# Three graph hops on one core: part of the row gather moved from GpSimd to SyncE, with a shorter ring of buffers

## The chip, the core and the metric

The program runs on one core of a Trainium2 chip. The core has TensorE (PE; its weight loads are listed as PEld), VectorE (DVE), ScalarE (ACT), GpSimd (POOL) and SyncE (SP), each with its own instruction stream; they meet through semaphores, and data moves between HBM and SBUF by DMA. The metric is device time of one execution, the median of several runs.

## The reference, cut to what matters

Four graph layers on 6250 nodes of 128 features and 100000 edges run one after the other. The first one holds the three hops of this case: a weighted sum over edges, three times (`Kh` is 4), each from the result of the last.

```python
edge_index = jnp.stack([src, dst])
row, col = (edge_index[0], edge_index[1])
def spmm(z):
    return jax.ops.segment_sum(edge_weight[:, None] * z[col], row, num_segments=N)
z = x
y = z @ weights[0]
for k in range(1, Kh):
    z = spmm(z)
    y = y + z @ weights[k]
return y / jnp.sqrt(jnp.asarray(d, dtype=x.dtype))
x = _layernorm(x + _L0_gnn_ref(x, edge_index, edge_weight, L0_gnn_weights), axis=-1)
```

Three attention layers follow, in which the destination-sorted and the source-sorted edge lists are used again.

## The kernel before, in words

**Lists.** The program first sorts the edges by `src` on the chip (`histogram`, `place_edges`, `scatter_edges`, `read_edges`). The sorted list is cut into chunks of 128 edges: 784 chunks (`CU`), of which 782 hold edges, in 196 groups of four (`GU`, `G`). `o.gather` holds, for each chunk, the node whose row each of its 128 edges needs. On the side of the sums there are 832 columns (`CH`) in 208 groups (`GROUPS`): a chunk that spans two blocks of 128 nodes is used by two columns. `o.chunk` says which chunk a column uses, `o.slot` where its rows lie in the ring, `o.need` up to which group of chunks it must have landed, and `o.free` how many groups of columns must be summed before a group of chunks is no longer needed.

**A hop** (`hop`, called three times) has five streams:

- POOL (L1117 to L1129) walks the 196 groups and issues four indirect DMAs in each, one a chunk: 128 rows of 512 bytes into one of 64 places of `rows`, a ring of 16 groups (`RING`). From group 16 on it first waits on `freed` for the group that held the place before.
- SP (L1314 to L1321) waits for each group to land (`got`), raises `landed` by one, and, from group 8 on, loads a number from `o.free`, waits on `summed` for the group eight back, and raises `freed`.
- PE (`a_round`, L1165 to L1190) waits for `landed` and for the weighted one-hot matrices, and multiplies four columns into PSUM.
- DVE makes these matrices (`weigh`, L1213) and adds the products to the block sums (`add`, L1226).
- In the first hop PE and DVE also count the keys of the second sort; in the second and third they also rank edges for it (`rank`), in the first 200 and 192 groups of columns.

```python
for n in range(GU):
    s = n % RING
    if n >= RING:
        pool.wait_ge(freed, n - RING + 1)
```

At the end of a hop DVE joins two half sums and SP stores the new table. The second hop's POOL stream then issues 16 scatter DMAs (L1136). After the third hop POOL goes straight on with the scatter of the second sort (`scatter_ranked`, L1355, 768 DMAs), beside the dense part of the first layer, and the list is read back after them.

**Order.** Each engine's order is the program's own; no planner sets it. Between the first sort and the scatter all engines meet at a block's end, and a hop starts behind such a meeting too: POOL begins its gathers right behind it, while PE, DVE, ACT and SP of the first two hops first finish a stage that they share the block with (`meet`, L75, and L1310 for SP).

Of the kernel before, what the change touches and what calls it, by code (L numbers as in the profile page):

```python
# [5 lines left out]
ALU = mybir.AluOpType  # L6
# [41 lines left out]
assert PAD_STEP * (CH - 1) + PAD_SKIP * (P - 1) < N  # L48
AFTER = NSLOT - E
assert TU * QU == CU and RING * G == 64 and NBLK < (RING - 2) * G  # L50

# [424 lines left out]
def place_edges(nc, k, counts, first_place, o, name, stack, shared):  # L476
# [18 lines left out]
    block_f = sb("block_f", [P, CH])  # L495
    row_i = sb("row_i", [1, CH], I32)
    need_i = sb("need_i", [1, GROUPS], I32)
    starts = ps("starts", [HIS, 1])
# [31 lines left out]
    def _(dve):  # L530
        steps = [0]

        def chain(ins):
            ins.then_inc(d, 1)
            steps[0] += 1
            dve.wait_ge(d, steps[0])
# [29 lines left out]
        nc.vector.tensor_scalar(o.block_base[:], block_f[:], float(P), None, ALU.mult)  # L566
        chain(nc.vector.tensor_copy(row_i[:], o.chunk[0:1, :]))
        chain(nc.vector.tensor_single_scalar(need_i[:], row_i[:, G - 1:CH:G], 2, ALU.arith_shift_right))
        nc.vector.tensor_single_scalar(o.slot[:], row_i[:], RING * G - 1, ALU.bitwise_and)
        nc.vector.tensor_scalar(o.need[:], need_i[:], 1.0, None, ALU.add)  # L570
        chain(nc.vector.tensor_single_scalar(block_f[:], block_f[:], float(NBLK - 1), ALU.min))
# [270 lines left out]
def read_edges(nc, k, table, o, name, stack, banks, shared):  # L842
# [23 lines left out]
    listed = sem("listed")  # L866
    limited = sem("limited")
    counted = sem("counted")
    counted_row = sem("counted_row")
# [11 lines left out]
    @shared.sync  # L881
    def _(sp):
        for h in range(2):
            here = slice(h * here_q, (h + 1) * here_q)
            sp.dma_start(lst[:, here, :], rows[:, here, :]).then_inc(loaded[h], 16)

    @shared.tensor
# [125 lines left out]
def hop(nc, k, o, table_in, table_out, name, tally=None, rank=None, shared=None, listed=None, early=None):  # L1013
# [3 lines left out]
    with ExitStack() as ctx:  # L1017
        sb, ps, sem = tools(nc, k, ctx, name)
        total = sb("total", [P, NBLK, D])
        odd = k.x[:, 0:NBLK, :]  # L1020
        rows = sb("rows", [P, RING * G, D])
        weighted = sb("weighted", [P, SLOTS, G, P])
        sums = ps("sums", [P, 2, G, D])
        got = [sem(f"got{s}") for s in range(RING)]
        landed = sem("landed")
# [4 lines left out]
        stored = sem("stored")  # L1030
        freed = sem("freed")
        running = sem("running")
        placed = sem("placed")
# [83 lines left out]
        def _(pool):  # L1117
            if listed is not None:
                pool.wait_ge(listed, 2)
            for n in range(GU):  # L1120
                s = n % RING
                if n >= RING:

                    pool.wait_ge(freed, n - RING + 1)
                    pool.sem_inc(running, 1)
                for g in range(G):
                    c = n * G + g
                    nc.gpsimd.indirect_dma_start(rows[:, s * G + g, :], None, table_in,  # L1128
                                                 bass.IndirectOffsetOnAxis(ap=o.gather[:, c:c + 1], axis=0),  # L1129
                                                 ).then_inc(got[s], 16)  # L1130
# [10 lines left out]
        def _(pe):  # L1141
# [26 lines left out]
            def a_round(i, first, ranks):  # L1168
                for s in range(DEEP):
                    b = s % 2  # L1170
                    n = i * DEEP + s
                    slots = load_blocks(nc, pe.engine, o.slot[:, bass.ds(n * G, G)], G, RING * G - 1)
                    need = pe.value_load(o.need[:, bass.ds(n, 1)], min_val=1, max_val=GU)
# [136 lines left out]
        @block.sync  # L1310
        def _(sp):
            home = table_out.rearrange("(b p) f -> p b f", p=P)
            for n in range(GU):
                sp.wait_ge(got[n % RING], (n // RING + 1) * 16 * G)  # L1314
                sp.sem_inc(landed, 1)  # L1315
                if n >= RING // 2 and n + RING // 2 < GU:

                    reader = sp.value_load(o.free[:, n - RING // 2:n - RING // 2 + 1], min_val=SLOTS + 1, max_val=GROUPS + SLOTS)
                    sp.wait_ge(summed, reader)
                    sp.sem_inc(freed, 1)  # L1320
            for n, here in enumerate(pieces):  # L1321
                sp.wait_ge(joined, n + 1)
                sp.dma_start(home[:, here, :], total[:, here, :]).then_inc(stored, 16)
            sp.wait_ge(stored, 16 * len(pieces))
# [1808 lines left out]
def graph_network(nc, a, out):  # L3133
    k = Shared()
    k.semaphores = []
    with ExitStack() as ctx:
# [17 lines left out]
        for o, n in ((by_src, "src"), (by_dst, "dst")):  # L3154
            o.place = sb(f"{n}_place", [P, CH + SPARE])
            o.begins = sb(f"{n}_begins", [P, CH], BF16)

            by_chunk = sb(f"{n}_by_chunk", [33, CH + SPARE], I32)
            o.block, o.within = by_chunk[0:1, :], by_chunk[32:33, :]
            o.sorted = dram(f"{n}_sorted", [LEAD + NSLOT + BEHIND, 4])  # L3160
            o.breaks = dram(f"{n}_breaks", [NSLOT + MOST_WCH * P], BF16)
        by_src.gather = sb("src_gather", [P, CU], I32)
        by_src.slot, by_src.need = sb("src_slot", [1, CH], I32), sb("src_need", [1, GROUPS], I32)
        by_src.free = sb("src_free", [1, 2 * P], I32)
        by_dst.typed = sb("dst_typed", [P, CH + SPARE], I32)
        by_dst.other = sb("dst_other", [P, CH + SPARE], I32)
# [10 lines left out]
        with ExitStack() as sort:  # L3177
# [8 lines left out]
            by_src.chunk_no = sort.enter_context(nc.sbuf_tensor("src_chunk_no", [P, QU], F32))  # L3186
            by_src.chunk = sort.enter_context(nc.sbuf_tensor("src_chunk", [P, CH], F32))
            with ExitStack() as unsorted:
                keys = unsorted.enter_context(nc.sbuf_tensor("keys", [P, 2, CH], F32))
# [142 lines left out]
```

## Time and profile before

| | |
|---|---|
| median of 3 runs | 9749.5 us (9728.2 to 9752.75) |
| profiled execution | 9737.26 us, span of the trace 9735.5 us |
| POOL busy | 6993.0 us, 72% of the span |
| DVE busy | 6539.5 us, 67% |
| PE busy | 6374.2 us, 65% |
| gathers of the three hops on POOL | 784 each |
| first gather of each hop | 1169.8, 2172.3 and 3185.0 us |

Register, branch, semaphore and DMA-issuing instructions of SP are not counted as busy, so SP has no line in the table of engines; its instructions are found by their lines. A POOL gather is counted as busy for the time in which POOL writes its DMA, not until the rows have landed. Idle time whose end is put down to "issue" is time in which an engine waited for nothing that the profile shows.

### The profile page before, as it was taken

The numbers are of one execution on the slowest core, as the hardware profiler recorded it, in microseconds if no ns is written. First come the engines' busy times: TensorE is split into PE (matmuls) and PEld (weight loads), VectorE is DVE, ScalarE is ACT, GpSimd is POOL, SyncE is SP. The second block draws the span as 40 slices with busy tenths as digits, with TensorE's granted clock in tenths as the row PEclk, the third lists the DMA queues.
The fourth block names the chain that finished last, engine by engine and source line by source line (L and its number), as shares of the span: only waits on it lengthen the run. The fifth ranks groups of instructions, "written<-read, shape, count | busy, mean of one in ns | idle before, by whom it ended". The sixth has DMA issues, their size and how long they took to land. (4 is left out here: it accounts for less than half of the span.)

```text
span 9735.5 us, 171552 instructions
## 1 busy us (share of the span) xinstructions
PE 6374.2 (65%) x37681; PEld 5551.4 (57%) x37682; DVE 6539.5 (67%) x22695; ACT 2118.1 (22%) x6216; POOL 6993.0 (72%) x7418
## 2 busy tenths in 40 slices
PE   6777655547666577639404666767776688876666
PEld 5666544436655566634204666556675578766665
DVE  7555566668777777736305888877777666667777
ACT  5222100001111111112101222232222222223333
POOL 7777777767777777777776777547775577767775
PEclk7555555556666655569756888889999665667777
DMA  0000012122212212234303333222222322223333
GB/s 25 2 2 2 18 53 52 53 61 53 53 53 55 57 53 53 53 77 146 100 2 86 104 104 104 87 47 55 55 55 55 100 54 54 54 72 108 108 108 97
DMA packets 436037, 614.74 MB, mean 63 GB/s; under 512 B 176561, under 2 KB 312069, under 8 KB 435109
## 3 DMA queue, kind: packets, MB, share of 16 engines
q0 software_dynamic: 257024, 486.93, 19.6%
q1 hardware_dynamic: 178305, 119.49, 4.3%
q8 instruction: 183, 3.00, 0.1%
q10 hardware_dynamic: 292, 3.41, 0.1%
q14 instruction: 233, 1.91, 0.1%
HBM read 520.17 MB, written 89.19 MB: 63 GB/s over the span
## 5 line engine op out<-in xcount | busy, mean ns | idle before, releaser
L1179 PE MATMUL hop_sums<-hop_rows,hop_weighted 128*128 x4992 | 1152.1, 403 | 1053.2 <-SPq L1315 674.4
L1128 POOL DMA_INDIRECT hop_rows<-hops,k_src_gather x1568 | 1483.3, 946 | 486.8 <-issue 477.6
L1179 PEld LDWEIGHTS hop_sums<-hop_rows,hop_weighted 128*128 128x128 f32 x4992 | 989.6, 295 | 1158.8 <-issue 1158.7
L1505 POOL DMA_INDIRECT l_pass_rows<-left_table,k_dst_other x832 | 796.2, 957 | 433.2 <-issue 244.6
L1505 POOL DMA_INDIRECT l_pass_rows<-related,k_dst_typed x832 | 788.6, 948 | 308.6 <-issue 238.7
L1505 POOL DMA_INDIRECT l_pass_rows<-key_table,k_src_gather x784 | 744.3, 949 | 365.9 <-issue 234.8
L2000 POOL DMA_INDIRECT l_weigh_rows<-row_table,l_weigh_ring x832 | 790.0, 949 | 297.9 <-issue 213.1
L728 POOL DMA_INDIRECT src_sorted<-src_scatter_records,src_scatter_places x784 | 753.1, 961 | 260.4 <-issue 188.2
L1355 POOL DMA_INDIRECT dst_sorted<-rec,dst_places x768 | 752.8, 980 | 237.2 <-issue 237.2
L1128 POOL DMA_INDIRECT hop_rows<-in_x,k_src_gather x784 | 742.4, 947 | 249.0 <-issue 238.7
L1213 DVE TENSOR_SCALAR hop_weighted<-k_numbers,k_src_place,src_weight 128x128 f32<-128x128 f32 x2496 | 850.1, 403 | 15.7 <-issue 8.7
L1521 ACT CAST l_pass_onehot_t<-l_pass_turned 128x512 f32<-128x512 bf16 x624 | 365.7, 586 | 2158.6 <-PE l_pass_turned L1569 2110.8
L1600 PE MATMUL l_pass_sums<-l_pass_zero 128*128 128x272 bf16 (+1 forms) x1210 | 235.7, 279 | 465.2 <-DVE l_total L1694 322.0
L1582 PE MATMUL l_pass_own<-l_right,l_pass_onehot_t 128*128 x1664 | 359.0, 299 | 257.7 <-DMA l_pass_rows<-left_table,k_dst_other 243.8
L1610 PE MATMUL l_pass_sums<-l_pass_terms,l_pass_onehot_f 128*128 128x136 f32 x3232 | 513.1, 308 | 1.1 <-DVE l_pass_terms L1877 1.1
L664 PE MATMUL src_scatter_nexts<-src_scatter_next_sb,src_scatter_oh_lo_t 128*128 128x50 f32 x1568 | 494.2, 425 | 0.0
L1106 ACT COPY hop_next_sb<-hop_next_ps 128x50 f32<-128x50 f32 x784 | 158.1, 202 | 1522.6 <-PE hop_next_ps L1151 1516.5
L1610 PEld LDWEIGHTS l_pass_sums<-l_pass_terms,l_pass_onehot_f 128*128 128x128 f32 x3232 | 472.1, 217 | 26.3 <-issue 3.2
L2018 PE MATMUL l_weigh_own<-l_keys,l_weigh_onehot_t 128*128 x1672 | 321.5, 352 | 229.9 <-ACT l_weigh_onehot_t L1970 229.9
L1814 DVE TENSOR_REDUCE l_pass_scores<-l_pass_pair 128x32 f32<-128x512 f32 (+1 forms) x624 | 426.2, 683 | 14.5
L1582 PEld LDWEIGHTS l_pass_own<-l_right,l_pass_onehot_t 128*128 128x128 f32 x1664 | 267.1, 202 | 289.7 <-issue 289.7
L2018 PEld LDWEIGHTS l_weigh_own<-l_keys,l_weigh_onehot_t 128*128 128x128 f32 x1672 | 272.4, 247 | 274.6 <-issue 274.6
(477 smaller groups left out, 17048.9 us busy)
## 6 DMA issues: line engine op xcount, KB each, us to landing
related<-l_tables_rows SPq DMA_DIRECT2D x50, 1024.0 KB, 4.5
hop_rows<-hops,k_src_gather POOLq DMA_INDIRECT x1568
l_pass_rows<-related,k_dst_typed POOLq DMA_INDIRECT x832
l_pass_rows<-left_table,k_dst_other POOLq DMA_INDIRECT x832
l_weigh_rows<-row_table,l_weigh_ring POOLq DMA_INDIRECT x832
src_sorted<-src_scatter_records,src_scatter_places POOLq DMA_INDIRECT x784, 2.1
hop_rows<-in_x,k_src_gather POOLq DMA_INDIRECT x784, 2.5
dst_sorted<-rec,dst_places POOLq DMA_INDIRECT x784
```

Source lines behind the costliest of these rows:

```text
L664: nc.tensor.matmul(nexts[:, b, g, 0:HIS], oh_lo_t[:, b, g, :], next_sb[:, g % 2, :], start=True, stop=True).then_inc(looked, 1)
L728: nc.gpsimd.indirect_dma_start(table, bass.IndirectOffsetOnAxis(ap=places[:, s, g:g + 1], axis=0), records[:, s, g, :], None).then_inc(sen ...
L1128: nc.gpsimd.indirect_dma_start(rows[:, s * G + g, :], None, table_in, bass.IndirectOffsetOnAxis(ap=o.gather[:, c:c + 1], axis=0),).then_in ...
L1179: last = nc.tensor.matmul(sums[:, b, g, :], weighted[:, s % SLOTS, g, :], rows[:, bass.ds(slots[g], 1), :], start=True, stop=True)
L1213: last = nc.vector.tensor_scalar(weighted[:, s, g, :], k.numbers, o.place[:, c], o.weight[:, c], ALU.is_equal, ALU.mult)
L1355: nc.gpsimd.indirect_dma_start(table, bass.IndirectOffsetOnAxis(ap=places[:, c:c + 1], axis=0), rec[:, c, :], None).then_inc(sent[c % SLOT ...
L1505: nc.gpsimd.indirect_dma_start(rows[:, s, g, :], None, table, bass.IndirectOffsetOnAxis(ap=index[:, c:c + 1], axis=0),).then_inc(got[s], 16)
L1582: last = nc.tensor.matmul(own[:, b, g, :], onehot_t[:, b, g, :], spread[:, bass.ds(blocks[g], 1), :], start=True, stop=(att is None))
L1610: last = nc.tensor.matmul(into[:, bass.ds(within[g], 1), 0:width], onehot_f[:, m % 2, g, :], term, start=False, stop=False, skip_group_che ...
L1814: nc.vector.tensor_reduce(mine, pair[:, b, :, :, :].rearrange("p (s t) h f -> p s t h f", t=per), AX.X, ALU.add).then_inc(scored, 1)
L2000: nc.gpsimd.indirect_dma_start(rows[:, s, g, :], None, table, bass.IndirectOffsetOnAxis(ap=ring[:, s, g:g + 1], axis=0),).then_inc(got[s], 16)
L2018: last = nc.tensor.matmul(own[:, b, g, :], onehot_t[:, b, g, :], spread[:, bass.ds(blocks[g], 1), :], start=True, stop=True)
```

## The change: what it does

In each hop, chunks 752 to 763 (groups 188 to 190, `AT_SIDE` to `BEHIND_SIDE`) are no longer gathered by POOL. Their 1536 rows are loaded by SP with one DMA of 512 bytes for each row, into 12 places of their own (`SIDE`) behind the ring. The node numbers for it are copied once, behind the first sort, from `o.gather` by way of HBM into one partition (`o.side`), and SP loads eight of them into registers at a time (`AT_ONCE`): a "part". There are 192 parts a hop: two behind each of groups 0 to 7 (`AHEAD`), then one behind each of groups 8 to 183. POOL also leaves out the last two chunks, which hold no edge: 770 gathers in place of 784. The ring has 8 groups in place of 16 (`NEAR`), and SP frees a group four behind the one that landed, not eight. `place_edges` works out a second table of places, `o.hop_slot`, for PE in the hops.

```diff
+CHUNKS = -(-E // P)
+NEAR = 8
+SIDE = 12
+AT_SIDE = 188
+BEHIND_SIDE = AT_SIDE + SIDE // G
+AT_ONCE = 8
+AHEAD = 8
...
-        chain(nc.vector.tensor_copy(row_i[:], o.chunk[0:1, :]))
+        chain(nc.vector.tensor_copy(row_i[:], o.chunk[:]))
...
+        chain(nc.vector.tensor_single_scalar(aside[:], row_i[:], AT_SIDE * G, ALU.is_ge))
+        chain(nc.vector.tensor_single_scalar(behind[:], row_i[:], BEHIND_SIDE * G, ALU.is_ge))
+        chain(nc.vector.tensor_tensor(aside[:], aside[:], behind[:], ALU.subtract))
+        chain(nc.vector.tensor_single_scalar(o.hop_slot, row_i[64:65, :], NEAR * G - 1, ALU.bitwise_and))
+        nc.vector.scalar_tensor_tensor(out=o.hop_slot, in0=aside[64:65, :], scalar=float(NEAR * G - AT_SIDE * G % (NEAR * G)),
+                                       in1=o.hop_slot, op0=ALU.mult, op1=ALU.add)
...
+        sp.wait_ge(listed, 2)
+        sp.dma_start(o.side_home, o.gather[:, AT_SIDE * G:BEHIND_SIDE * G]).then_inc(side_in, 16)
+        sp.wait_ge(side_in, 16)
+        sp.dma_start(o.side[:], o.side_home.rearrange("(a p) c -> a (p c)", a=1)).then_inc(side_in, 16)
+        sp.wait_ge(side_in, 32)
...
-        rows = sb("rows", [P, RING * G, D])
+        rows = sb("rows", [P, NEAR * G + SIDE, D])
...
-            for n in range(GU):
-                s = n % RING
-                if n >= RING:
-
-                    pool.wait_ge(freed, n - RING + 1)
+            for n in [*range(AT_SIDE), *range(BEHIND_SIDE, GU)]:
+                s = n % NEAR
+                if n >= NEAR:
+
+                    before = n - NEAR if not AT_SIDE <= n - NEAR < BEHIND_SIDE else n - 2 * NEAR
+                    pool.wait_ge(freed, before + 1)
                     pool.sem_inc(running, 1)
-                for g in range(G):
+                for g in range(min(G, CHUNKS - n * G)):
...
+            order = [(p, c) for p in range(P) for c in range(SIDE)]
+            used = [0] * NEAR
             for n in range(GU):
-                sp.wait_ge(got[n % RING], (n // RING + 1) * 16 * G)
+                if AT_SIDE <= n < BEHIND_SIDE:
+                    for part in range(SIDE // 2 if n == AT_SIDE else 0):
+                        sp.wait_ge(side_got[part], 16 * 2 * P)
+                else:
+                    used[n % NEAR] += 16 * min(G, CHUNKS - n * G)
+                    sp.wait_ge(got[n % NEAR], used[n % NEAR])
                 sp.sem_inc(landed, 1)
-                if n >= RING // 2 and n + RING // 2 < GU:
-
-                    reader = sp.value_load(o.free[:, n - RING // 2:n - RING // 2 + 1], min_val=SLOTS + 1, max_val=GROUPS + SLOTS)
+                done = n - NEAR // 2
+                if 0 <= done < AT_SIDE:
+
+                    reader = sp.value_load(o.free[:, done:done + 1], min_val=SLOTS + 1, max_val=GROUPS + SLOTS)
                     sp.wait_ge(summed, reader)
                     sp.sem_inc(freed, 1)
+                for part in (2 * n, 2 * n + 1) if n < AHEAD else (n + AHEAD,):
+                    mine = order[part * AT_ONCE:(part + 1) * AT_ONCE]
+                    if not mine:
+                        continue
+                    nodes = load_blocks(nc, sp.engine, o.side[:, part * AT_ONCE:(part + 1) * AT_ONCE], AT_ONCE, N - 1)
+                    for e, ((p, c), node) in enumerate(zip(mine, nodes)):
+                        sp.dma_start(rows[p:p + 1, NEAR * G + c, :], table_in[bass.ds(node, 1), :],
+                                     ).then_inc(side_got[(part * AT_ONCE + e) // (2 * P)], 16)
```

SP's stream at the start of the first hop, before; `src_read_lst` is the sorted list being read back, and each pair of rows from L1318 on is one step of freeing a group (waits and moves of a register are not listed):

```order
L885 DMA src_read_lst<-src_sorted 98x4x512 x2
L121 UNCONDITIONAL_BRANCH
L1310 UNCONDITIONAL_BRANCH
L1318 TENSOR_LOAD k_src_free
L1318 ISA x2
```

The same place now; `src_side` are the node numbers of the rows that SP loads, and the two last rows are one row's address and its DMA:

```order
L902 DMA src_read_lst<-src_sorted 98x4x512 x2
L904 DMA src_side_home<-k_src_gather 128x12
L906 DMA src_side<-src_side_home 1x1536
L129 UNCONDITIONAL_BRANCH
L1334 UNCONDITIONAL_BRANCH
L139 TENSOR_LOAD src_side
L1359 ISA
L1359 DMA hop0_rows<-in_x 1x128
```

Two copies come ahead of the hop, and the first loads of rows come ahead of the first freeing. Further on, from group 8 to group 183, one step of SP reads as follows; the pair of L1359 stands eight times in each step, and once here:

```order
L1350 TENSOR_LOAD k_src_free
L1350 ISA x2
L139 TENSOR_LOAD src_side
L1359 ISA
L1359 DMA hop0_rows<-in_x 1x128
```

Where a step had one load and two register instructions, it now has one load, eight addresses and eight DMAs more. DVE's stream in `place_edges`, before, with `row_i` the chunk of each column as a whole number:

```order
L567 CAST src_base_row_i<-src_chunk 1x832
L568 TENSOR_SCALAR src_base_need_i<-src_base_row_i 1x208
L569 TENSOR_SCALAR k_src_slot<-src_base_row_i 1x832
L570 TENSOR_SCALAR k_src_need<-src_base_need_i 1x208
L571 TENSOR_SCALAR src_base_block_f<-src_base_block_f 128x832
```

The same place now, where `k_src_by_chunk` in L583 and L584 is `o.hop_slot`:

```order
L577 CAST src_base_row_i<-src_chunk 128x832
L578 TENSOR_SCALAR src_base_need_i<-src_base_row_i 128x208
L579 TENSOR_SCALAR k_src_slot<-src_base_row_i 1x832
L580 TENSOR_SCALAR src_base_aside<-src_base_row_i 128x832
L581 TENSOR_SCALAR src_base_behind<-src_base_row_i 128x832
L582 TENSOR_TENSOR src_base_aside<-src_base_aside,src_base_behind 128x832
L583 TENSOR_SCALAR k_src_by_chunk<-src_base_row_i 1x832
L584 SCALAR_TENSOR_TENSOR k_src_by_chunk<-src_base_aside,k_src_by_chunk 1x832
L586 TENSOR_SCALAR k_src_need<-src_base_need_i 1x208
L587 TENSOR_SCALAR src_base_block_f<-src_base_block_f 128x832
```

Five instructions are new, L580 to L584. POOL's stream differs only in the count of its gathers, 770 a hop.

## Rows read from the trace of the kernel before

**Rows 1.** Stretches of the three hops' gathers: span, each engine's busy time, clock, DMA.
```profile
core 0: us, PE busy (x) PEld busy (x) DVE busy (x) ACT busy (x) POOL busy (x), PEclk, DMA share, GB/s
1170.00:2150.00 980.00, 529.05 (x2526) 436.55 (x2525) 665.86 (x2090) 0.00 (x0) 741.27 (x784) 0.54 0.20 53
2172.00:3153.00 981.00, 649.53 (x3668) 595.57 (x3668) 749.75 (x3580) 150.48 (x602) 741.97 (x785) 0.66 0.20 53
3185.00:4166.00 981.00, 676.64 (x3582) 622.85 (x3581) 734.70 (x3490) 144.65 (x578) 741.95 (x785) 0.59 0.20 53
```

**Rows 2.** Costliest groups, the page's part 5: count, busy, mean ns, idle before.
```profile
L1128 POOL DMA_INDIRECT hop_rows<-hops,k_src_gather x1568 | 1483.3, 946 | 486.8 <-issue 477.6
L1355 POOL DMA_INDIRECT dst_sorted<-rec,dst_places x768 | 752.8, 980 | 237.2 <-issue 237.2
```

**Rows 3.** SP's waits, 1230 to 2150 us: line, what for, us, times, longest.
```profile
SPq L1315 <- DMA hop_rows<-in_x,k_src_gather: 800.1, 184, 5.1
```

**Rows 4.** L1128 from each hop's start through group 12: ns min/median/max, first and last start.
```profile
L1128 POOL DMA_INDIRECT hop_rows<-in_x,k_src_gather x49: 941/947/1573, 1169.8 to 1230.8; - x49
...
DMA to landing us min/median/max: 2.4/2.5/3.3
...
L1128 POOL DMA_INDIRECT hop_rows<-hops,k_src_gather x49: 941/947/1365, 2172.3 to 2232.8; - x49
...
L1128 POOL DMA_INDIRECT hop_rows<-hops,k_src_gather x49: 941/947/983, 3185.0 to 3245.1; - x49
```

**Rows 5.** L1315, SP's first step in each hop, columns as in rows 4.
```profile
L1315 SPq EVENT_SEMAPHORE  x3: 17/17/17, 1182.1 to 1187.2; - x3
...
L1315 SPq EVENT_SEMAPHORE  x1: 17/17/17, 2181.1 to 2181.1; - x1
...
L1315 SPq EVENT_SEMAPHORE  x1: 17/17/17, 3191.4 to 3191.4; - x1
```

**Rows 6.** One freeing step of SP, 1602.3 us: L1315, L1318 (all 540), L1320.
```profile
L1315 SPq EVENT_SEMAPHORE  x1: 17/17/17, 1602.3 to 1602.3; - x1
...
L1318 SPq TENSOR_LOAD <-k_src_free x540: 262/267/465, 1217.1 to 4126.8; - x180
L1318 SPq FUSED_REGOPS  x540: 147/147/190, 1217.6 to 4127.1; - x180
L1318 SPq SEQ_ASSERT  x540: 18/18/33, 1217.9 to 4127.3; - x180
...
L1320 SPq EVENT_SEMAPHORE  x1: 17/17/17, 1602.9 to 1602.9; - x1
```

**Rows 7.** L1479, SP's DMAs of four partitions in a run, columns as in rows 4.
```profile
L1479 SPq DMA_DIRECT2D l_pass_brk<-dst_breaks x35: 268/298/343, 6429.2 to 6440.9; - x35
```

**Rows 8.** L2436, SP's DMAs whose address is in a register, 128 partitions.
```profile
L2436 SPq FUSED_REGOPS  x50: 46/46/51, 4422.6 to 4732.1; - x50
L2436 SPq MOVE related<-l_tables_rows x50: 29/29/29, 4422.7 to 4732.2; - x50
L2436 SPq DMA_DIRECT2D related<-l_tables_rows x50: 372/372/409, 4422.7 to 4732.3; - x50
```

**Rows 9.** L2579, a run of 128-partition DMAs on SP (one of six), columns as in rows 4.
```profile
L2579 SPq DMA_DIRECT2D k_bias<-in_L_gnn_bo x1: 432/432/432, 4391.7 to 4391.7; - x1
```

**Rows 10.** Timeline of ACT's DMA queue at 138 us; L295 moves one row: start, us.
```profile
138.44 0.30 ACTq L295 DMA_DIRECT2D dst_sorted<-dst_load_pad  x1
```

**Rows 11.** POOL's gathers at 7609 to 7633 us, while SP issues DMAs, columns as rows 2.
```profile
L1505 POOL DMA_INDIRECT l_pass_rows<-key_table,k_src_gather x20 | 18.9, 946 | 133.0 <-POOLq L2614 127.2 <-issue 5.8
```

**Rows 12.** SP's DMA queue in the same stretch: start, us.
```profile
7608.47 23.78 SPq L1479 DMA_DIRECT2D l_pass_brk<-src_breaks  x32
```

**Rows 13.** DVE in `place_edges`, 149 to 154 us, columns as in rows 2.
```profile
L574 DVE TENSOR_TENSOR k_src_by_chunk<-src_base_block_f 1x832 int32<-1x832 f32 x1 | 1.0, 1016 | 0.0
...
L569 DVE TENSOR_SCALAR k_src_slot<-src_base_row_i 1x832 int32<-1x832 int32 x1 | 0.6, 580 | 0.0
```

**Rows 14.** POOL's end of the second hop, 3150 to 3190 us, columns as in rows 2.
```profile
L1136 POOL DMA_INDIRECT dst_sorted<-rec,dst_places x16 | 18.1, 1129 | 4.9 <-issue 4.9
```

More of the change, by code:

```diff
@@ L49 @@
 AFTER = NSLOT - E
+CHUNKS = -(-E // P)
[5 more added lines that the diff above has]
+AHEAD = 8
+assert SIDE * P <= AT_ONCE * (AT_SIDE - 2 + AHEAD) and AT_SIDE * G % (NEAR * G) + SIDE <= NEAR * G and SIDE // G <= NEAR // 2 and BEHIND_SIDE + NEAR >= GU - 1
 assert TU * QU == CU and RING * G == 64 and NBLK < (RING - 2) * G
@@ L495, in place_edges @@
     block_f = sb("block_f", [P, CH])
-    row_i = sb("row_i", [1, CH], I32)
-    need_i = sb("need_i", [1, GROUPS], I32)
+    row_i = sb("row_i", [P, CH], I32)
+    aside = sb("aside", [P, CH], I32)
+    behind = sb("behind", [P, CH], I32)
+    need_i = sb("need_i", [P, GROUPS], I32)
     starts = ps("starts", [HIS, 1])
@@ L566, in _ @@
         nc.vector.tensor_scalar(o.block_base[:], block_f[:], float(P), None, ALU.mult)
-        chain(nc.vector.tensor_copy(row_i[:], o.chunk[0:1, :]))
+        chain(nc.vector.tensor_copy(row_i[:], o.chunk[:]))
         chain(nc.vector.tensor_single_scalar(need_i[:], row_i[:, G - 1:CH:G], 2, ALU.arith_shift_right))
-        nc.vector.tensor_single_scalar(o.slot[:], row_i[:], RING * G - 1, ALU.bitwise_and)
-        nc.vector.tensor_scalar(o.need[:], need_i[:], 1.0, None, ALU.add)
+        nc.vector.tensor_single_scalar(o.slot[:], row_i[0:1, :], RING * G - 1, ALU.bitwise_and)
+        chain(nc.vector.tensor_single_scalar(aside[:], row_i[:], AT_SIDE * G, ALU.is_ge))
[4 more added lines that the diff above has]
+                                       in1=o.hop_slot, op0=ALU.mult, op1=ALU.add)
+        nc.vector.tensor_scalar(o.need[:], need_i[0:1, :], 1.0, None, ALU.add)
         chain(nc.vector.tensor_single_scalar(block_f[:], block_f[:], float(NBLK - 1), ALU.min))
@@ L867, in read_edges @@
     limited = sem("limited")
+    side_in = sem("side_in")
     counted = sem("counted")
@@ L1020, in hop @@
         odd = k.x[:, 0:NBLK, :]
-        rows = sb("rows", [P, RING * G, D])
+        rows = sb("rows", [P, NEAR * G + SIDE, D])
         weighted = sb("weighted", [P, SLOTS, G, P])
         sums = ps("sums", [P, 2, G, D])
-        got = [sem(f"got{s}") for s in range(RING)]
+        got = [sem(f"got{s}") for s in range(NEAR)]
         landed = sem("landed")
@@ L1031, in hop @@
         freed = sem("freed")
+        side_got = [sem(f"side_got{n}") for n in range(SIDE // 2)]
         running = sem("running")
@@ L1171, in a_round @@
                     n = i * DEEP + s
-                    slots = load_blocks(nc, pe.engine, o.slot[:, bass.ds(n * G, G)], G, RING * G - 1)
+                    slots = load_blocks(nc, pe.engine, o.hop_slot[:, bass.ds(n * G, G)], G, NEAR * G + SIDE - 1)
                     need = pe.value_load(o.need[:, bass.ds(n, 1)], min_val=1, max_val=GU)
@@ L3156, in graph_network @@
             o.begins = sb(f"{n}_begins", [P, CH], BF16)
-            by_chunk = sb(f"{n}_by_chunk", [33, CH + SPARE], I32)
-            o.block, o.within = by_chunk[0:1, :], by_chunk[32:33, :]
+            by_chunk = sb(f"{n}_by_chunk", [65, CH + SPARE], I32)
+            o.block, o.within, o.hop_slot = by_chunk[0:1, :], by_chunk[32:33, :], by_chunk[64:65, 0:CH]
             o.sorted = dram(f"{n}_sorted", [LEAD + NSLOT + BEHIND, 4])
@@ L3164, in graph_network @@
         by_src.free = sb("src_free", [1, 2 * P], I32)
+        by_src.side_home = dram("src_side_home", [P, SIDE], I32)
         by_dst.typed = sb("dst_typed", [P, CH + SPARE], I32)
@@ L3187, in graph_network @@
             by_src.chunk = sort.enter_context(nc.sbuf_tensor("src_chunk", [P, CH], F32))
+            by_src.side = sort.enter_context(nc.sbuf_tensor("src_side", [1, P * SIDE], I32))
             with ExitStack() as unsorted:
```

## The prediction, made before the changed kernel ran

> **What bounds the kernel now.** I read the stretches of the three hops first, then the costliest groups, then what SP waits for, and last SP's single instructions, since they are what the change adds.
>
> In a hop POOL does nothing but gather. The stretches have 784 gathers each in 980 us [rows 1], and the group of L1128 has 1483.3 us busy and 477.6 us of "issue" for 1568 gathers [rows 2]: 1.251 us a gather, 5.00 us a group of four, with next to no waiting. SP waits 800.1 us of the 920 us read for gathers to land [rows 3], so SP, PE and DVE follow POOL. DVE is busy 666 to 750 us of each 980 [rows 1]; it keeps pace. Behind the third hop POOL goes on with 768 scatters, again with "issue" as its only idle time [rows 2], so what POOL gains or loses in a hop is carried to the end.
>
> What the ring costs now can be read at a hop's start. POOL's first gather comes at 1169.8, 2172.3 and 3185.0 us, and the 49th, the first of group 12, at 1230.8, 2232.8 and 3245.1: 61.0, 60.5 and 60.1 us later [rows 4], no stall. SP's first step stands at 1182.1, 2181.1 and 3191.4 [rows 5]: 12.3, 8.8 and 6.4 us after the first gather.
>
> **The gain.** POOL issues 14 gathers fewer in each hop: 14 x 1.251 = 17.5 us, 52.5 us in all three. That is the most that the change can give.
>
> **The cost of a step of SP.** A freeing step runs from 1602.3 to 1602.9 us [rows 6]. Its four instructions ahead of L1320 last 0.017, 0.267, 0.147 and 0.018 us, 0.45 together, so some 0.04 us lies between two. With L1320 itself the step is 0.66 us. In a run of small DMAs the starts are (6440.9 - 6429.2) / 34 = 0.344 us apart at 0.298 us each [rows 7], so a gap of 0.045 us. A DMA with its address in a register takes a register operation of 0.046 us and a MOVE of 0.029 us ahead of it [rows 8]. A row on SP is then 0.086 + 0.069 + D + 0.045 = 0.20 + D us, where D is the DMA instruction. A part of eight rows is a load (0.31) and eight rows: 1.91 + 8 D.
>
> No row shows D for one row on SP with its address in a register. From below: a DMA of four partitions took 0.268 us at the least [rows 7]; nothing excludes less for one row, down to the 0.046 of a register operation [rows 8]. From above: the same DMAs in a close run 0.298 [rows 7], one row on ACT's queue right behind a large DMA 0.30 [rows 10], 128 partitions 0.372 alone and 0.432 in a run [rows 8, 9]. I take 0.268: few partitions, and 0.2 us of other work ahead of each, so no close run. That the address is in a register seems free: 0.372 for 128 partitions [rows 8] is below the 0.432 of fixed addresses [rows 9].
>
> A row then costs 0.468, a part 4.05, and a step from group 8 on 0.66 + 4.05 = 4.71 us, under POOL's 5.00: hidden, by a narrow margin. D may be 0.304 before the step passes 5.00.
>
> The freeing step rests on a register load of 0.267 us [rows 6]. The Trainium skill, in "DMA: Bandwidth & Descriptors", section "Latency and other measured facts", gives a floor of about 600 ns for such a load; by that, both loads of a step would be 0.33 us longer, the step 5.37 us, and SP would hold POOL back by about 0.37 us x 176 steps x 3 hops = 195 us more, with 21 us more at the starts. The trace's 0.267 us is the measurement, and decides.
>
> **The start of a hop.** Here the cover is missing. With a ring of 8, POOL needs the first freed group at its group 8, and the n-th at group 7 + n. SP frees the first in its step of group 4, and each of its first eight steps carries two parts, 8.10 us. Steps 0 to 3 take 8.16 us, steps 4 to 7 8.76, and the fifth freeing is done 4 x 8.16 + 4 x 8.76 + 0.66 = 68.3 us after SP's first step. POOL waits for it at group 12: 12.3 + 68.3 - 61.0 = 19.6 us late in the first hop, 16.6 in the second, 14.6 in the third, 50.8 in all. From there POOL's 5.00 is again the longer step, and the lateness stays. Queued behind SP's parts are `landed`, which PE then sees late, and `freed`; PE and DVE have nothing to do meanwhile and catch up.
>
> **The side groups.** POOL's group 191 follows 187 and uses the place of 183, which SP frees only after 187 has landed. A gather lands 2.5 us after its issue [rows 4], SP frees 0.6 later, and POOL was ready 1.25 after that issue: 1.9 us a hop, 5.7 in all. The side rows are issued by step 183, some 20 us ahead of their use. Their own landing is hidden.
>
> **Outside the hops.** Five DVE instructions are chained in `place_edges`, on the way to the first scatter: three like L569's 0.58 us, two like L574's 1.02 [rows 13], with 0.03 us between them 3.9 us. Nothing hides them. The two copies of the node numbers lie beside the stage that SP waits for until its first step at 1182.1 [rows 5], 12.3 us after the list is ready: two landings of some 2.5 us and their issues fit, so nothing. In the second hop POOL's 16 scatters [rows 14] move with its gathers. SP's DMAs do not slow POOL's gathers: while SP issued 32 of them in 23.78 us [rows 12], 20 gathers took 0.946 us with 5.8 us of issue between them [rows 11], as in the hops. If that cover fails, each 0.01 us a gather costs 770 x 3 x 0.01 = 23 us.
>
> **The sum.** -52.5 + 50.8 + 5.7 + 3.9 = +7.9 us on 9737.26: 9745 us for the profiled execution. It lies 12.2 us under the median of 9749.5, inside the runs' spread, so the median is forecast at 9757.5 us. In D the sum is 384 D - 94.7, as long as SP's step is under 5.00 and each start is late.
>
> **The rivals.**
> 1. SP becomes the bound (slower). If a row DMA takes over 0.304 us, each of the 176 steps from group 8 on is longer than POOL's 5.00 and POOL waits on `freed` all through: each 0.01 us more costs 8 x 176 x 3 x 0.01 = 42 us, beside the starts. At 0.30 us [rows 10] the sum is +20, still hidden; at 0.33 it is 32 + 110 = +142; at 0.432 [rows 9] +612. For it: 0.298 in a close run [rows 7] is already near the point. Against it: the 0.2 us between two DMAs, and one row in place of four. The Trainium skill speaks for the far end: its table of DMA instructions ("DMA: Bandwidth & Descriptors", section "Why a DMA increments its semaphore by 16 and not by 1") gives 512 cycles for a copy before the newest generation, and "Trainium Kernel Development and Optimization", "NeuronCore Architecture", 1.2 GHz for SyncE, an estimate of 0.43 us whatever the shape. The trace agrees for 128 partitions [rows 9] and not for four [rows 7]. Chance of D over 0.306: 0.24, of the far end 0.03 of it.
> 2. A row is cheap (faster). With D under 0.17 the starts cost 14 us or less and the sum is under -29; with no lateness at all it is -43 (9706.5). For it: the time falls with the number of partitions, 0.432 or 0.372 against 0.268 [rows 7 to 9]. Against it: nothing shown is under 0.268. Chance 0.10.
> 3. The sums come in a heap at the end. When group 187 has landed, PE and DVE have the three side groups and POOL's last five to do, 8.5 groups of columns, in the 24 us that POOL's 18 gathers take. At DVE's mean of 3.2 to 3.6 us a group (666 to 750 us over 208) [rows 1] that is 27 to 31 us, 3 to 6 us late in each hop, +15 in all: +23. Against it: the last eight groups carry no ranking, and the mean contains it. Chance 0.08, inside "no change".
> 4. The change doesn't free POOL as it says: POOL's group 12 waits on PE, not on SP. PE's sums would have to be four groups late; SP's steps of before never waited long on them (0.66 us from landing to freed) [rows 6]. Under 0.02.
>
> **How the numbers follow.** A measurement of this kernel tells a change from none at about 0.3%, 29 us. The forecast with rival 3, D between 0.17 and 0.306, holds 0.66: no change. Rival 1 holds 0.24: slower. Rival 2 holds 0.10: faster. The likeliest case alone runs from 9721 to 9779. The range of 8 in 10 goes from 9723 (D of 0.18) up to 9850 (D of 0.321, +100), past which half of rival 1 remains.
>
> **What would show it.** In the changed profile the row DMAs on SP should take about 0.27 us and their starts lie 0.47 apart; a step 4.7 us; POOL's 49th gather should come 80, 77 and 75 us after its first, and the 752nd to 753rd show 1.9 us of idle time; between them 1.251 us a gather. POOL's first scatter of the first sort should come 3.9 us later. If POOL waits on SP at every group, rival 1 holds; if the 49th gather comes at 61 us, rival 2. A gather cadence away from 1.251 us, or a gap between the hops that grows by more than 5 us, would break the sum elsewhere.

## The result, and the profile after

The changed kernel took 9767.5 us (median of 14 runs, 9761.0 to 9783.0), the kernel before 9744.7 on the same chip (14 runs, among them the three of the table above): a ratio of 1.0027, 95% interval 1.0018 to 1.0035. That is inside the 0.3% that the prediction called no change, though the interval lies above 1: the change did cost time. The median is 10 us above the forecast; the shift from the kernel before is 22.8 us in place of the 7.9 forecast, since the kernel before came out 4.8 us lower in 14 runs than in three. The profiled execution took 9766.7 us, with a span of 9765.0.

The costliest group that answers to the first of [rows 2], with the second and third hop's gathers:

```profile
L1152 POOL DMA_INDIRECT hop_rows<-hops,k_src_gather x1540 | 1453.5, 944 | 523.2 <-issue 422.3
```

Of the idle time some 100 us now have another releaser than "issue" (before 9.2): 91.3 us are waits for SP's L1352. POOL's gathers of each whole hop, changed kernel (columns as in [rows 4]):

```profile
L1152 POOL DMA_INDIRECT hop_rows<-in_x,k_src_gather x770: 938/944/1573, 1169.0 to 2156.4; - x193
...
L1152 POOL DMA_INDIRECT hop_rows<-hops,k_src_gather x770: 938/944/1358, 2179.4 to 3162.6; - x193
...
L1152 POOL DMA_INDIRECT hop_rows<-hops,k_src_gather x770: 938/944/980, 3195.7 to 4177.5; - x193
```

The same in a second profile of the kernel before:

```profile
L1128 POOL DMA_INDIRECT hop_rows<-in_x,k_src_gather x784: 940/944/1570, 1164.4 to 2142.8; - x196
...
L1128 POOL DMA_INDIRECT hop_rows<-hops,k_src_gather x784: 940/944/1352, 2165.2 to 3143.0; - x196
...
L1128 POOL DMA_INDIRECT hop_rows<-hops,k_src_gather x784: 940/944/980, 3176.1 to 4153.6; - x196
```

Why a second profile: POOL's pace differs a little between executions. In the first one of before a gather took 0.947 us in the median [rows 4] and came every 1.251 us, in both profiles here 0.944 and 1.249. Over 784 gathers that is 1.6 us, so hops are compared at one pace. With 14 gathers fewer the stretches went from 978.4, 977.8 and 977.5 us to 987.4, 983.2 and 981.8: 9.0, 5.4 and 4.3 us longer, 18.7 in all. (A second profile of the changed kernel at 1.251, against the first of before, gives 18.7 as well.)

The start of each hop, which answers to [rows 4], with what POOL's idle time waited for below each (us, times):

```profile
L1152 POOL DMA_INDIRECT hop_rows<-in_x,k_src_gather x49: 938/944/1573, 1169.0 to 1253.5; - x49
...
  SPq L1352: 25.0, 5
...
L1152 POOL DMA_INDIRECT hop_rows<-hops,k_src_gather x49: 938/944/1358, 2179.4 to 2259.7; - x49
...
  SPq L1352: 21.5, 5
...
L1152 POOL DMA_INDIRECT hop_rows<-hops,k_src_gather x49: 938/944/980, 3195.7 to 3273.6; - x49
...
  SPq L1352: 19.5, 5
```

The 49th gather comes 84.5, 80.3 and 77.9 us after the first, against 61.0, 60.5 and 60.1 [rows 4]: 23.5, 19.8 and 17.8 us late, 61.1 in all. In between it waits five times, at groups 8 to 12, for L1352, SP's raise of `freed`. SP's side of the first hop, its steps 0 to 8:

```profile
L1346 SPq EVENT_SEMAPHORE  x9: 17/17/17, 1181.4 to 1251.6; - x9
```

That is 70.2 us for eight steps with two parts each; in the other hops they take 69.9. The other place is POOL's 753rd gather, first of group 191, in its timeline (start, duration):

```profile
2131.22 0.94 POOL L1152 DMA_INDIRECT hop_rows<-in_x,k_src_gather  x1 [0.30 <-issue]
2135.17 0.94 POOL L1152 DMA_INDIRECT hop_rows<-in_x,k_src_gather  x1 [3.01 <-SPq L1352]
```

It is 3.95 us behind the one before it, 2.7 too much; in the other hops 2.8 and 3.6. Against [rows 3], SP now waits for landings hardly at all in the same stretch:

```profile
SPq L1346 <- DMA hop_rows<-in_x,k_src_gather: 34.6, 52, 4.7
```

34.6 us in place of 800.1. SP's instructions, loads of row numbers first in steps 0 to 3, then from 1300 to 1500 us, the load of `o.free` in the latter, the same behind the last parts, and the row DMAs:

```profile
L139 SPq TENSOR_LOAD <-src_side x8: 708/799/942, 1181.4 to 1211.3; - x8
...
L139 SPq TENSOR_LOAD <-src_side x41: 524/528/531, 1301.3 to 1495.9; - x41
...
L1350 SPq TENSOR_LOAD <-k_src_free x42: 442/459/615, 1300.5 to 1499.8; - x42
...
L1350 SPq TENSOR_LOAD <-k_src_free x4: 262/266/282, 2133.8 to 2136.0; - x4
...
L1359 SPq DMA_DIRECT2D hop_rows<-hops x3072: 224/225/322, 2189.0 to 4138.6; - x192
...
L1359 SPq DMA_DIRECT2D hop_rows<-in_x x8: 224/225/269, 1506.5 to 1509.4; - x8
```

The row DMA takes 0.225 us, and eight of them stand (1509.4 - 1506.5) / 7 = 0.41 us apart. The load of `o.free` takes 0.266 us where no DMA was issued just ahead of it (as in [rows 6]) and 0.459 right behind the DMAs of a part. SP's steps from 1300 to 1500 us:

```profile
L1346 SPq EVENT_SEMAPHORE  x42: 17/17/17, 1300.4 to 1499.8; - x42
```

A step is (1499.8 - 1300.4) / 41 = 4.86 us, against POOL's 4 x 1.249 = 5.00 a group. SP works its backlog off: its step of a group comes 30.5 us after that group's last gather was issued at group 8, 13.8 at group 12 and 2.5, the time of a landing, at group 112.

### The profile page after: what moved, and what is told of

Its sections match the earlier page's. It is cut to its first block and busy times, and to the rows that moved or that the text cites. A ratio compares the mean times of both kernels' runs of the same rounds, so it can differ in the third digit from the quotient of the medians.

```text
span 9765.0 us, 186035 instructions
## 1 busy us (share of the span) xinstructions
PE 6408.4 (66%) x37681; PEld 5581.8 (57%) x37682; DVE 6547.5 (67%) x22700; ACT 2116.8 (22%) x6216; POOL 6934.4 (71%) x7376
## 5 line engine op out<-in xcount | busy, mean ns | idle before, releaser
L1152 POOL DMA_INDIRECT hop_rows<-hops,k_src_gather x1540 | 1453.5, 944 | 523.2 <-issue 422.3
L1545 POOL DMA_INDIRECT l_pass_rows<-left_table,k_dst_other x832 | 794.4, 955 | 434.7 <-issue 243.1
L2040 POOL DMA_INDIRECT l_weigh_rows<-row_table,l_weigh_ring x832 | 786.8, 946 | 316.5 <-issue 212.5
L1545 POOL DMA_INDIRECT l_pass_rows<-related,k_dst_typed x832 | 786.3, 945 | 311.5 <-issue 235.2
L1545 POOL DMA_INDIRECT l_pass_rows<-key_table,k_src_gather x784 | 742.8, 947 | 369.9 <-issue 228.3
L1237 DVE TENSOR_SCALAR hop_weighted<-k_numbers,k_src_place,src_weight 128x128 f32<-128x128 f32 x2496 | 850.1, 403 | 13.5 <-issue 8.4
L1177 PE MATMUL hop_nexts<-hop_next_sb,hop_oh_lo_t 128*128 128x50 f32 x1568 | 437.4, 377 | 0.0
```

The source lines that it names most:

```text
L1177: nc.tensor.matmul(nexts[:, b, g, 0:HIS], oh_lo_t[:, b, g, :], next_sb[:, g % 2, :], start=True, stop=True).then_inc(looked, 1)
L1237: last = nc.vector.tensor_scalar(weighted[:, s, g, :], k.numbers, o.place[:, c], o.weight[:, c], ALU.is_equal, ALU.mult)
L1545: nc.gpsimd.indirect_dma_start(rows[:, s, g, :], None, table, bass.IndirectOffsetOnAxis(ap=index[:, c:c + 1], axis=0),).then_inc(got[s], 16)
L2040: nc.gpsimd.indirect_dma_start(rows[:, s, g, :], None, table, bass.IndirectOffsetOnAxis(ap=ring[:, s, g:g + 1], axis=0),).then_inc(got[s], 16)
```

## The experiments

The theory that was tested (A): POOL sets the time of a hop; SP falls behind in its first eight steps, and POOL pays for that where the ring runs out. The rival (B): 1536 rows are more than SP can carry beside its freeing.

**A longer ring, 12 chunks as in the change.** For room, the node numbers lie, in two halves, in partition 96 of two tiles that are there anyway.

```diff
-NEAR = 8
+NEAR = 16
...
-            by_src.side = sort.enter_context(nc.sbuf_tensor("src_side", [1, P * SIDE], I32))
+            by_src.side = (by_src.spare_row, by_dst.spare_row)
```

> The changed kernel with a ring of 16 groups again (SP frees eight behind), the same 12 chunks on SP; the node numbers lie in two spare partitions so that it fits. Theory A (the 12 chunks' gain is lost at each hop's start, where SP does two parts a group and POOL's group 8 needs SP's fifth step): POOL is not late at group 12 (first gather to 49th 61, 60.5, 60 us, not 84, 80, 78), the stall ahead of group 191 is gone, a hop's gathers take 963 to 968 us, and the median is 40 to 50 us under the kernel before. Theory B (SP's steps are too long all through a hop, whatever the ring): hops stay near 985 us and the time within 10 us of the changed kernel.

Missed: 9755.7 us against 9730.4 of before, 1.0026 (1.0017 to 1.0035), no better than the change. The start did go well (49th gather at 61.0, 60.3 and 60.0 us), but the time came back. SP's loads of row numbers and its steps from 1300 to 1500 us, and under them POOL's timeline at its 753rd gather:

```profile
L139 SPq TENSOR_LOAD <-k_src_by_chunk x288: 682/686/935, 1183.7 to 3679.1; - x144
...
L1347 SPq EVENT_SEMAPHORE  x40: 17/17/17, 1301.7 to 1497.7; - x40
```

```profile
2117.07 0.94 POOL L1153 DMA_INDIRECT hop_rows<-in_x,k_src_gather  x1 [0.30 <-issue]
2132.84 0.94 POOL L1153 DMA_INDIRECT hop_rows<-in_x,k_src_gather  x1 [14.83 <-SPq L1353]
```

A step of SP that waits for nothing is (1497.7 - 1301.7) / 39 = 5.03 us, longer than POOL's 5.00. SP's step of group 8 in the first hop comes 35 us after that group's last gather was issued, and its step of group 183 still 34 us. POOL then waits 14.8 us for a place, and the sums that were announced late follow after the last gather: from there to the next hop's first gather it takes 37.8 us, where before took 22.4. The ring only moved the price. The load of 0.686 us in place of 0.528 was my own doing.

**The short ring alone**: POOL gathers all 782 chunks, SP none.

```diff
...
-            for n in [*range(AT_SIDE), *range(BEHIND_SIDE, GU)]:
+            for n in range(GU):
...
-                for part in (2 * n, 2 * n + 1) if n < AHEAD else (n + AHEAD,):
+                for part in ():
```

> The ring of 8 alone: POOL gathers all 782 chunks, SP loads no rows. Theory A: nothing is late, a hop's gathers take 977 us (two gathers fewer), the time is 5 to 10 us under the kernel before. Rival, the short ring itself holds POOL back (PE's sums are not done in time): the 49th gather is late as in the changed kernel and the time is 10 to 25 us over the kernel before. If the rest of the program (not the hops) is some 10 us longer here too, that loss belongs to the list stage or the layout and not to SP's loads.

9724.9 us, 0.9993 (0.9984 to 1.0002), 5.4 us under before, which the interval does not tell from no change. The profile does. POOL's waits for SP in all three hops:

```profile
POOL hop_rows L1152 <- SPq L1348: 6.1, 20, 0.3
```

None is longer than the 0.3 us that stand between any two gathers. The hops' gathers take 977.8, 977.3 and 976.9 us, 2.4, 2.3 and 2.4 less than in the first profile of before, which ran at the same pace of 1.251: two gathers fewer. A ring of 8 costs nothing by itself.

**Eight chunks, one part behind each of groups 0 to 127.**

```diff
-SIDE = 12
+SIDE = 8
...
-AHEAD = 8
+AHEAD = 0
```

> The changed kernel with 8 chunks on SP in place of 12, one part behind each of groups 0 to 127 and none doubled; ring of 8; POOL gathers 774. Theory A: SP's first steps are 4.1 to 5 us, the fifth freeing comes in time, the 49th gather 61 us after the first, a hop 967 us, and the median 30 to 42 us under the kernel before, although SP does less for POOL. Theory B: SP is as late as before in groups 0 to 127 and the time stays within 10 us of the kernel before.

9696.6 us, 0.9963 (0.9950 to 0.9977), as expected. POOL's waits for SP in all three hops:

```profile
POOL hop_rows L1152 <- SPq L1352: 58.8, 193, 0.3
```

Again none is over 0.3 us. The hops' gathers take 966.0, 965.6 and 965.1 us, 37.0 less than before at the same pace, where ten gathers fewer are 10 x 1.249 x 3 = 37.5. But B is not excluded: these are also fewer rows.

**Two loads of four numbers per part.**

```diff
-                    nodes = load_blocks(nc, sp.engine, o.side[:, part * AT_ONCE:(part + 1) * AT_ONCE], AT_ONCE, N - 1)
...
+                        if e % 4 == 0:
...
+                            nodes = load_blocks(nc, sp.engine, o.side[:, at:at + 4], 4, N - 1)
```

> The changed kernel with two loads of four node numbers for each part in place of one of eight: some 0.55 us more in each part of SP. Theory A with SP's margin read from the changed trace (a step of 4.9 us against POOL's 5.0): the step passes POOL's, POOL waits on SP at every group, 0.45 us x 176 x 3 = 240 us, and some 27 us more at the starts: 260 to 290 us over the changed kernel. Rival (SP has slack to spare after the start, and the loads hide): under 40 us over the changed kernel, from the starts alone.

9927.4 us, 1.0200 (1.0181 to 1.0219). Its loads, and its steps, from 1300 to 1500 us:

```profile
L139 SPq TENSOR_LOAD <-src_side x76: 297/424/697, 1300.7 to 1499.8; - x76
...
L1346 SPq EVENT_SEMAPHORE  x38: 17/17/17, 1303.3 to 1498.6; - x38
```

The step is 195.3 / 37 = 5.28 us, and POOL follows SP all through: the three stretches are 163 us longer than the changed kernel's. The mechanism is as expected, the size smaller, some 174 us over the changed kernel's excess in place of 260 to 290: two loads of four make the step of 4.86 only 0.42 us longer. The rival's 40 us are excluded.

**The same 12 chunks, spread evenly**: parts of 16 rows, one behind about every second group. In a second run SP also frees a group three behind the landed one.

```diff
-AT_ONCE = 8
+AT_ONCE = 16
...
-                for part in (2 * n, 2 * n + 1) if n < AHEAD else (n + AHEAD,):
+                for part in [k for k in range(SIDE * P // AT_ONCE) if k * (AT_SIDE - 6) // (SIDE * P // AT_ONCE) == n]:
```

The second run besides:

```diff
-                done = n - NEAR // 2
+                done = n - 3
```

> The changed kernel with the same 12 chunks, but no two parts behind a group at the start: 96 parts of 16 rows, one behind about every second of groups 0 to 180. Theory A (SP falls behind in its first eight steps, of two parts each, and that backlog is what the change pays): SP never falls behind by more than a part, POOL's 49th gather comes 61, 60 and 60 us after the first as before, the only stall left is the one before group 191 (2.7 to 3.6 us), so a hop's gathers take 770 x 1.249 + 3 = 965 us, 15 less than before, 45 in three hops; 35 to 45 us under the kernel before, ratio 0.9955 to 0.9965. Rival B (12 chunks are more than SP can carry, and eight chunks gained because they are fewer rows): POOL still waits on SP, within 10 us of the kernel before or slower.

> The run with parts of 16 rows spread evenly, and besides SP frees a group three behind the one that landed, not four. Theory A: the stall before group 191 goes, since the place of group 183 is freed a group earlier, 2.7 to 3.6 us a hop, some 9 us in all below that run; 45 to 55 us under the kernel before, ratio 0.9945 to 0.9955. Rival: the sums are not three groups behind in time, SP waits on PE in its freeing steps, and the landed groups are announced late; no gain over that run, or a loss, and waits on PE in SP's list.

9695.2 and 9684.5 us against 9732.5 of before: 0.9960 (0.9947 to 0.9974) and 0.9955 (0.9941 to 0.9968). B falls: these are the change's 1536 rows. The parts are larger too, but that is worth little. In the first of the two SP's loads of 16 numbers take

```profile
L139 SPq TENSOR_LOAD <-src_side x288: 965/973/1207, 1183.7 to 4061.0; - x144
```

0.973 us, against 2 x 0.528 for two loads of eight: 0.08 us less in 16 rows. POOL's group 191 in the first of the two, and the second one's gathers of whole hops:

```profile
2109.95 0.94 POOL L1152 DMA_INDIRECT hop_rows<-in_x,k_src_gather  x1 [0.30 <-issue]
2113.96 0.94 POOL L1152 DMA_INDIRECT hop_rows<-in_x,k_src_gather  x1 [3.07 <-SPq L1352]
```

```profile
L1152 POOL DMA_INDIRECT hop_rows<-in_x,k_src_gather x770: 940/944/1572, 1171.6 to 2132.7; - x193
...
L1152 POOL DMA_INDIRECT hop_rows<-hops,k_src_gather x770: 940/944/1352, 2158.4 to 3118.9; - x193
...
L1152 POOL DMA_INDIRECT hop_rows<-hops,k_src_gather x770: 940/944/980, 3152.7 to 4112.8; - x193
```

In the first the stall ahead of group 191 is left, as expected. In the second it is gone, and the stretches are 961.1, 960.5 and 960.1: 52.0 us less than before, the whole of 14 x 1.249 x 3 = 52.5. SP does wait on PE there, but little:

```profile
SPq L1352 <- PE hop_sums L1203: 9.5, 6, 3.6
```

That the second is faster than the first is shown by the stretches (8.6 us); the intervals of the two times overlap.

**Eight chunks with the change's start**, and the same with a ring of 16 (numbers in their own tile).

```diff
-AHEAD = 0
+AHEAD = 8
```

The second run besides:

```diff
-NEAR = 8
+NEAR = 16
```

> The run with eight chunks on SP, and again two parts behind each of groups 0 to 7, then one behind each of groups 8 to 119. The rows are the same as in that run, only their order is not. Theory A: POOL's 49th gather comes 84, 80 and 78 us after its first, as in the changed kernel; about 58 us over the run with eight chunks spread evenly, 15 to 25 us over the kernel before, ratio 1.0015 to 1.003. Rival B (the number of rows counts, not where they stand): within 10 us of that run, 30 us under the kernel before.

> The same eight chunks with two parts behind each of groups 0 to 7, and a ring of 16 groups in place of eight (SP frees eight behind). Theory A in its new form (a backlog of SP costs where the ring runs out, and nothing where SP can work it off before): SP is some 32 us behind until group 119, has no parts from there on and catches up; POOL's 49th gather comes 61 us after its first and no stall over 3 us stands in a hop; 30 to 35 us under the kernel before, ratio 0.9960 to 0.9970. Rival (the longer ring itself costs what the run with 12 chunks and 16 groups lost): as slow as the kernel before or slower, at 1.001 to 1.003.

9760.9 us, 1.0030 (1.0018 to 1.0042), and 9697.3, 0.9964 (0.9950 to 0.9977). The first hop's start and its waits in the first of them:

```profile
L1152 POOL DMA_INDIRECT hop_rows<-in_x,k_src_gather x49: 940/944/1570, 1170.0 to 1254.5; - x49
...
  SPq L1352: 25.1, 5
```

With the order of the rows alone the 23.5 us came back, and the three stretches are 61.2 us longer than with the even spread. In the other run POOL's waits for SP and SP's steps from 1300 to 1500 us:

```profile
POOL hop_rows L1152 <- SPq L1352: 27.3, 87, 1.0
```

```profile
L1346 SPq EVENT_SEMAPHORE  x41: 17/17/17, 1301.3 to 1496.0; - x41
```

No wait is over 1.0 us. A step is 194.7 / 40 = 4.87 us, so SP gains on POOL: its step comes 35 us after the last gather at group 8 and 21 at group 119. From group 120 on it has no parts, and by group 130 it is level. In this run a backlog cost nothing: the ring bridged it, and SP had time to work it off.

**The changed kernel with its numbers in partition 96**, ring of 8.

> The changed kernel, ring of 8 and all, with the node numbers of SP's rows in partition 96 of a tile that is there anyway, where the run with 16 groups had them, in place of a tile of their own from partition 0. Theory: a load of eight numbers from there takes 0.686 us in place of 0.528 (as in that run), so the 16 parts of a hop's first eight steps take 2.5 us more, and a step that waits for nothing goes from some 4.87 to 5.02 us, past POOL's 4.996: SP never works off the 14 us that it is behind at group 12, and POOL waits at every group, some 0.03 us x 176 = 5 us a hop; 20 to 25 us over the changed kernel, ratio to the kernel before 1.004 to 1.006. Rival (the 0.16 us are hidden, and the 16 groups lost their gain by something else): within 5 us of the changed kernel, 1.002 to 1.003.

9778.1 us, 1.0047 (1.0031 to 1.0064) to before, some 22 us over the changed kernel's excess. Its load takes 0.686 us, and its steps from 1300 to 1500 us:

```profile
L1347 SPq EVENT_SEMAPHORE  x40: 17/17/17, 1303.9 to 1500.0; - x40
```

5.03 us, as in the run with 16 groups; SP's step comes 14.4 us after the last gather at group 12 and 13.5 at group 183. One part was off: a start lost only 0.7 us more, not 2.5. Of the first 16 loads only the four right behind a freeing step differ, 0.68 to 0.69 us against 0.53; the others take 0.71 to 0.95 with either place.

**Further profiles of both kernels**, for a stretch outside the change: from the third attention layer's last gather (L1545, before L1505) to the next stage's first (L2040, L2000), 64.4 us in the changed kernel's profile and 45.5 in that of before.

> The changed kernel once more, for its profile: the hops should again lose 13 us by the end of the third gather. The time from the last gather of the third attention layer's POOL stage to the first of the stage behind it was 64.4 us in the first profile and 45.5 us in that of the kernel before. If that is chance, it comes somewhere between 45 and 65; if it belongs to the change, over 60.

> The kernel before once more, for its profile: the same stretch behind the third layer's gathers. If the 45.5 us were chance, it comes between 45 and 65; if the change lengthens it, 44 to 48.

> The kernel before a third time, for the same stretch and with the same two outcomes: between 45 and 65 if it is chance, 44 to 48 if the change lengthens it.

The changed kernel again, then the kernel before again:

```profile
L1545 POOL DMA_INDIRECT l_pass_rows<-key_table,k_src_gather x784: 942/947/1347, 7631.3 to 8618.2; - x196
...
L2040 POOL DMA_INDIRECT l_weigh_rows<-row_table,l_weigh_ring x832: 942/949/1016, 8667.1 to 9708.4; - x167
```

```profile
L1505 POOL DMA_INDIRECT l_pass_rows<-key_table,k_src_gather x784: 940/944/1272, 7596.8 to 8578.7; - x196
...
L2000 POOL DMA_INDIRECT l_weigh_rows<-row_table,l_weigh_ring x832: 942/946/1080, 8637.8 to 9676.7; - x167
```

48.9 us for the change, 59.1 for before, and 54.0 in the third profile of before. The second pair has the two kernels the other way round, so the 19 us don't belong to the change; a single pair of profiles would have laid them to it.

## Why the prediction came out as it did

The forecast and its mechanism held: the gain of 14 gathers a hop is real, and SP's first eight steps give it back. The sum was +7.9 us; with the measured terms it is +22.6, and the median moved by 22.8.

| term | forecast | measured |
|---|---|---|
| 14 gathers fewer | -52.5 | -52.0, in the run without stalls |
| starts of the hops | +50.8 | +61.1 |
| stall ahead of group 191 | +5.7 | +9.1 |
| `place_edges` | +3.9 | +3.7 |
| between the hops | 0 | +0.7 |
| sum | +7.9 | +22.6 |

The term that was mis-sized is the starts of the hops, 61.1 us for 50.8, and after it the stall. One omission stands in both "The start of a hop" and "The side groups": they end with SP's raise of `freed`, and left out that POOL's next gather starts 0.8 us later. In the changed kernel's first hop, the raises behind groups 8 and 187 (the second row's first raise is that for an earlier group), and the same in the third hop:

```profile
L1352 SPq EVENT_SEMAPHORE  x1: 17/17/17, 1252.7 to 1252.7; - x1
...
L1352 SPq EVENT_SEMAPHORE  x2: 17/17/17, 2129.4 to 2134.4; - x2
...
L1352 SPq EVENT_SEMAPHORE  x2: 17/17/17, 4149.5 to 4155.4; - x2
```

The gathers that they released start at 1253.5, 2135.17 and 4156.2; in all 18 long waits of the three hops it is 0.81 us. For the stall in the first hop that is all: 2.5 of landing, 0.6 of freeing, 0.8, less 1.25, is 2.7. In the third hop group 187's last gather landed 3.4 us after its start in place of 2.5, which makes its 3.6.

For the starts the larger part is another: eight steps of two parts took longer than forecast. Of the 3.9 us that were missing in the first hop, they are 2.5 (70.2 us against 4 x 8.16 + 4 x 8.76 = 67.7), the raise 0.8, and the ninth step's freeing 0.5, 1.1 us from 1251.6 to 1252.7 against 0.66.

- **D** was 0.225 us, not 0.268, and a row 0.41, not 0.468. A part came out near its 4.05 us all the same, because its load was 0.53 to 0.94 us and not 0.267: two errors that cancel, which is luck. With the measured D alone the prediction's 384 D - 94.7 gives -8.3 us, further from what came than with 0.268. The load of one number in [rows 6] was the wrong row for a load of eight behind DMAs. The Trainium skill's floor of about 600 ns for such a load ("DMA: Bandwidth & Descriptors", section "Latency and other measured facts") is not a floor here, at 0.266 us, but nearer for the loads that the change added than the row that I took.
- **A steady step** was 4.86 us, not 4.71: hidden, as forecast, with 0.13 us to spare and not 0.29.
- **Rival 1** (SP the bound) did not occur, but the margin was as narrow as claimed: the runs with 0.16 and 0.42 us more a step crossed it. Its cause, a long row DMA, was the wrong one to fear; the loads are what can push SP over.
- **Rival 2** (cheap rows): D came out between the forecast's 0.268 and the 0.17 that this rival needed, and the kernel was not faster, because rows are not all of a part.
- **Rival 3** (a heap of sums at the end) did not show in the change: from the last gather to the next hop's first it takes 23.0 and 33.1 us, before 22.4 and 33.1. It showed where SP stayed 34 us behind, with 37.8.
- **Rival 4** is out: POOL's long waits inside a hop are all for SP, and SP's own list of waits has none on PE in its freeing steps.
- **`place_edges`**: the first scatter starts at 164.4 us in the mean over eleven profiles with the new lines, 160.7 over three of before. The single profiles spread by 4.0 and 3.0 us, so it is the five instructions themselves that carry this term: 0.58, 0.59, 1.03, 0.58 and 1.02 us, 3.80 in all.

## What to carry to other kernels

An idle engine can take work from a bound one, but its backlog has to be followed through the loop: work placed in a lump at the start, with a ring too short to bridge it, gave back all that the moved work had won. The same rows spread evenly kept most of it (43.4 of 52.5 us in the three stretches), and all once a group was freed one earlier (52.0; 0.9955 of the kernel before). A longer ring paid where a step of the helper, all its instructions counted, stayed below the leader's (4.87 against 5.00, eight chunks); at 5.03 it moved the price to the end. Twelve chunks with a ring of 16 and the shorter load were not run. And where a wait is released by another engine, the time from the raise to the released work's start belongs in the sum.

## What the runs showed of the hardware

- A register load on SP cost more with more numbers and behind DMAs: one number 0.266 us, or 0.459 right behind row DMAs; four 0.30 or 0.55; eight 0.528 right behind a freeing step, and 0.71 to 0.94 in a hop's first four steps; sixteen 0.973. Eight numbers from partition 96 of another tile took 0.686 where those of their own tile took 0.528, and no more than those in the first four steps. Whether it is the partition or the place within it was not tried.
- A DMA of one row on SP took 0.225 us to issue, under the 0.268 to 0.298 of four partitions [rows 7], though its address came from a register.
- POOL's pace differed between executions by 0.2% (1.249 or 1.251 us a gather), enough to blur a difference of a few us a hop.
- From SP's raise of a semaphore to the start of the POOL gather that waited for it: 0.81 us, in all 18 long waits of the changed kernel's hops.
- SP's steps came in two lengths, 4.78 and some 5.13 us, about one in four the longer. The longer ones hold a gap: after every 128 of SP's recorded instructions the trace has 0.33 to 0.35 us without an instruction (from 1501.75 to 1502.08 us, say), 19 times from 1300 to 1700 us, some 21 us apart and at any place of a step. By an estimate from these numbers (0.34 / 128) each instruction on SP costs 0.003 us beside its own time. Three such gaps are some 1 us of the first eight steps' 70.2. What SP does in the gap the trace does not show.
